# Loading the key blocks of a batch: four 32-partition transfers with a repeated source for eight of 16 partitions

## The chip, the cores and the metric

The kernel runs on one core of a Trainium2 chip. The metric is the device time of one execution in microseconds (us). The engines are TensorE (PE in the profile), VectorE (DVE), ScalarE (ACT), GpSimd (POOL) and SyncE (SP); PEld is TensorE's weight load. SP issues every transfer of this kernel, on one queue; the transfers run on 16 DMA engines. A statement of no change means within 2%.

## What is computed

Eight batches of 512 tokens with 256 features go through cross attention to 64 context tokens, and then through a mixture of eight experts. Cut to what matters:

```python
Q = (layernorm(x) @ WQ + bQ).reshape(b, 16, -1, 16)      # 16 heads of 16 features
K = (ctx @ WK + bK).reshape(b, 16, -1, 16)
V = (ctx @ WV + bV).reshape(b, 16, -1, 16)
attn = softmax(einsum('bhqd,bhkd->bhqk', Q, K) * mask) / 4
x = x + merge_heads(attn @ V) @ Wp + bp
# router: softmax over 8 experts of layernorm(x) * gamma + beta
# expert 0 has the given W1, b1, W2, b2; experts 1 to 7 share one perturbed copy
x = x + sum_e prob_e * (gelu(x @ W1_e + b1_e) @ W2_e + b2_e)
```

The experts take x as it is; only the router takes the normalised x, scaled by gamma and shifted by beta. The perturbed weights need two ranks (the largest and the smallest 5% by magnitude), which the kernel finds by a bit-by-bit search.

## The kernel before

The five engines have one hand-written program each, and semaphores join them. The main part is a loop over the eight batches (`body`, called by `pipeline`): step i finishes the attention of batch i, runs the first expert of batch i-1 beside it, does some steps of the rank search, and prepares the queries and the first three quarters of the attention scores of batch i+1. After the loop (`last_expert`) the weights are perturbed, and the second expert runs over all batches on its own.

**Where the change sits.** The scores of a batch need a block matrix of its keys, `kbd`, with 128 partitions. Its 128 rows are eight blocks of 16 rows: block 2h+n belongs to head h of a group of four. The queries were split into a high and a low part, and both parts meet the same keys; so block 2h and block 2h+1 hold the same 16 rows of `kh_scr` in HBM, at the same columns (64 to a head, for 4 groups and 2 parts of the keys: 8 runs of 64 numbers, or 256 bytes, in each row). What lies beside the blocks is zero from the start and stays so.

**SP's order.** In each step SP calls `store_queries(i+1)`, four stores of the queries to HBM (`q_scr`, L397); `load_queries(i+1)`, two loads of them in another layout (`qs`, L404), which wait until the stores have landed; and `load_context(i+1)` (L407), which loads the key blocks (`kbd`, L412), then the mask (`mk`, L416, four transfers) and the values (`vbd`, L419, two). Then come the store of the turned activations (`xt_scr`, L493) and others; the key loads of batch 0 are issued ahead of the loop. SP issues in this order, one after the other.

**Who waits for them.** `scores(b, j)` on PE (L553) waits at j = 0 for `q_in` and for `k_in`, all of a batch's key transfers. It is followed in PE's program by `router` (L637), the rest of the first expert of batch i-1 (`hidden`, `output`) and `scores(i+1, 1)` and `scores(i+1, 2)`. PE runs its instructions in order, so these stand behind the wait. `mask_scores(b, j)` on DVE (L1171) multiplies the scores with the mask and waits at j = 0 for `mask_in`; `shift` (POOL, L1062), `probs` (ACT, L866) and `turn_probs` (PE, L582) follow it. `values` (PE, L604) waits until all of a batch's scores are masked. At the switch between two rounds of the rank search DVE has a stretch of work of its own (`second_round`, L1302): between steps 2 and 3.

Of the kernel before, what the change touches and what calls it, by code (L numbers as in the profile page):

```python
# [8 lines left out]
F32 = mybir.dt.float32  # L9
# [29 lines left out]
def build_program(nc, x, ctx_in, mask, WQ, bQ, WK, bK, WV, bV, Wp, bp,  # L39
                  W1, b1, W2, b2, gamma, beta, Wr, br, out):  # L40
    B, S, D = x.shape
    CT = ctx_in.shape[1]
# [3 lines left out]
    DK = D // H  # L46
# [3 lines left out]
    HH = H // 2  # L50
# [4 lines left out]
    HG = H // 4  # L55
# [14 lines left out]
    def sb(name, shape, dt=F32):  # L70
        return ctx.enter_context(nc.sbuf_tensor(name, shape, dt))

    def sig(name, per=1):
        return Signal(ctx.enter_context(nc.semaphore(name)), per)
# [13 lines left out]
    kh_scr = nc.dram_tensor("kh_scr", [B, 4 * DK, HG, 2, CT], F32, kind="Internal").ap()  # L88
# [4 lines left out]
    def view(region, start, *shape):  # L93

        n = 1
        for d in shape:
            n *= d
        ap = region[:, start:start + n]
        if len(shape) == 1:
            return ap  # L100
        names = "abc"[:len(shape)]
        return ap.rearrange("p (" + " ".join(names) + ") -> p " + " ".join(names), **dict(zip(names[1:], shape[1:])))
# [15 lines left out]
    g = view(region_b, 2 * DC * S, 4, S)  # L118
# [68 lines left out]
    kbd = sb("kbd", [P, HG, 2, 4 * CT], F32R)  # L187
# [77 lines left out]
    keep_in = sig("keep_in", 16)  # L265
    mask_in = sig("mask_in", 16 * CC)
    v_in = sig("v_in", 32)
    k_in = sig("k_in", 16 * HH)
    q_out = sig("q_out", 2 * 16 * DC)
    q_in = sig("q_in", 2 * 16)  # L270
    ln = [dict(stats=sig(f"ln{n}_stats", NT), mean=sig(f"ln{n}_mean", NT), var=sig(f"ln{n}_var", 2),
# [50 lines left out]
    def by_query(ap, cc):  # L322

        return ap.rearrange("(r j cc) d -> cc r j d", j=NT, cc=CC)[cc]
# [24 lines left out]
    def wait(eng, signal, batch, count=None):  # L349


        value = signal.at(batch, count)
        if value > 0:
            eng.wait_ge(signal.handle, value)
# [26 lines left out]
    def _(sp):  # L381
# [25 lines left out]
        def load_context(b):  # L407
            wait(sp, s_product, b - 1)
            for h in range(4):
                for n in range(2):  # L410
                    row = (2 * h + n) * DK
                    sp.dma_start(kbd[row:row + DK, :, :, CT * h:CT * h + CT].rearrange("p g n k -> p (g n) k").bitcast(F32),  # L412
                                 kh_scr[b, DK * h:DK * h + DK].rearrange("d g n k -> d (g n) k")).then_inc(k_in.handle, 16)
            wait(sp, s_masked, b - 1)
            for cc in range(CC):
                sp.dma_start(mk[cc * R:(cc + 1) * R], by_query(mask[b], cc)).then_inc(mask_in.handle, 16)  # L416
            wait(sp, o_product, b - 1)
            for o in range(2):
                sp.dma_start(vbd[CT * o:CT * o + CT, :, DK * o:DK * o + DK],  # L419
                             v_scr[b].rearrange("t (c d) -> (t c) d", d=DK).rearrange("(g o k) d -> o k g d", k=CT, o=2)[o]).then_inc(v_in.handle, 16)  # L420
# [50 lines left out]
        sp.wait_ge(kv_out, 32)  # L471
        sp.wait_ge(eye_ready, 3)
        load_context(0)

        def put_expert(b):
# [3 lines left out]
        def body(i, rnd, first=False, last=False):  # L479
            if i + 2 < B:  # L480
                load_x(i + 2)
            load_residual(i)
            if not last:
                store_queries(i + 1)
                load_queries(i + 1)
                load_context(i + 1)
            else:

                wait(sp, o_product, i)
                sp.dma_start(wagain[:, 0].rearrange("p (c f) -> p c f", c=DC), W1.rearrange("(c p) f -> p c f", p=P)).then_inc(ld_again, 16)  # L490
                sp.dma_start(wagain[:, 1].rearrange("p (c d) -> p c d", c=FC), W2.rearrange("(c p) d -> p c d", p=P)).then_inc(ld_again, 16)
            wait(sp, x2T_ready, i)
            sp.dma_start(xt_scr[i], x2T.rearrange("p c s -> p (c s)")).then_inc(x2T_out.handle, 16)  # L493
            wait(sp, x2_ready, i)
            wait(sp, ex[0]["mixed"], i - 1)
            sp.dma_start(keep[:], x2[:]).then_inc(keep_in.handle, 16)
            if not first:
                put_expert(i - 1)
# [1062 lines left out]
```

## Time and profile before

| | |
|---|---|
| median of 3 runs | 804.89 us (800.08 to 814.68) |
| the profiled execution | 803.5 us |
| its span, first to last instruction | 801.7 us |
| granted TensorE clock, mean | 0.882 |

The span is the profiled execution without 1.8 us around it. The loop over the batches fills it from about 60 to 575 us; the second expert takes the rest. The chain of waits is followed back from the last instruction; "issue" in it is time in which an engine waited for nothing that the profile shows. A row of the timeline gives the start in us, the length in us, the engine, the line, the operation, what it writes and reads, how many instructions are merged in it, and in brackets how long the engine was idle before it and what released it.

### The profile page before, as it was taken

How to read it: one execution, taken by the hardware profiler on the slowest of the kernel's cores; microseconds unless marked ns; L12 is line 12 of the kernel's file. 1: busy time of each engine (PE TensorE's matmuls, PEld its weight loads, DVE VectorE, ACT ScalarE, POOL GpSimd, SP SyncE). 2: the span in 40 equal slices, each digit the busy share in tenths (PEclk: the TensorE clock that was granted, in tenths of full speed). 3: DMA queues.
4: the chain of work that ended last, by engine and by line, in shares of the span. 5: the costliest groups of instructions: out<-in, count | busy, mean ns of one | idle time of the engine just before them, and what ended most of it. 6: DMA issues, size and time to landing. Idle time of an engine off the chain costs nothing.

```text
span 801.7 us, 13910 instructions
## 1 busy us (share of the span) xinstructions
PE 683.7 (85%) x5442; PEld 566.5 (71%) x5442; DVE 514.0 (64%) x988; ACT 369.3 (46%) x544; POOL 228.3 (28%) x210
## 2 busy tenths in 40 slices
PE   5457777998995799898898898899987999999995
PEld 4346576886784687687687677668765888888884
DVE  5879768759669865965865874866497343343441
ACT  2214235546554554555454644545533544455442
POOL 2224034354244244334325424514280000000000
PEclk9758658989998898998797898869898999999998
DMA  9951342333153051342324206130102112222211
GB/s 279 164 134 25 54 129 54 54 102 106 19 138 105 2 111 45 107 81 75 107 38 117 80 9 147 61 124 29 68 12 80 27 53 79 80 79 79 79 32 48
DMA packets 133041, 64.40 MB, mean 80 GB/s; under 512 B 105712, under 2 KB 123120, under 8 KB 132976
## 3 DMA queue, kind: packets, MB, share of 16 engines
q1 hardware_dynamic: 132976, 63.51, 30.4%
q8 instruction: 43, 0.70, 0.4%
q14 instruction: 22, 0.18, 0.1%
HBM read 36.21 MB, written 23.09 MB: 74 GB/s over the span
## 4 chain that ended last, share of the span: by engine, by line
PE 60%; DVE 20%; issue 6%; ACT 4%; DMA 4%; SPq 3%; POOL 1%; DVEq 0%; ACTq 0%; POOLq 0%
PE ps_y L340 6%; PE ps_y L341 6%; PE ps_y L342 6%; PE ps_h L340 5%; PE ps_h L342 5%; PE ps_h L341 5%; DVE region_a L1171 3%; PE ps_t L340 3%; DVE ind L1269 3%; PE ps_m L688 3%; PE ps_t L341 3%; PE ps_t L342 3%; PE ps_t L582 3%; PE ps_t L637 2%; ACT region_a L871 2%
## 5 line engine op out<-in xcount | busy, mean ns | idle before, releaser
L1080 POOL TENSOR_TENSOR region_c_lo<-region_b,region_c_hi 128x512 fp32r<-128x512 f32 x64 | 95.7, 1504 | 117.2 <-ACT region_c_hi L910 117.2
L907 ACT ACTIVATE region_b<-ps_h,bias 128x512 f32<-128x512 f32 x92 | 63.2, 687 | 117.9 <-PE ps_h L342 116.9
L1532 DVE TENSOR_TENSOR region_c_lo<-region_b,region_c_hi 128x512 fp32r<-128x512 f32 x64 | 44.1, 692 | 107.8 <-ACT region_c_hi L910 107.8
L1269 DVE TENSOR_SCALAR ind<-key,cand 128x2048 bf16<-128x2048 uint16 x124 | 100.1, 849 | 18.2 <-PE ps_m L688 17.3
L340 PE MATMUL ps_y<-region_c_hi,w_hi 128*128 128x512 f32 x256 | 106.3, 415 | 1.9 <-POOL region_c_lo L1080 1.6
L341 PE MATMUL ps_y<-region_c_lo,w_hi 128*128 128x512 f32 x256 | 103.5, 404 | 0.0
L342 PE MATMUL ps_y<-region_c_hi,w_lo 128*128 128x512 f32 x256 | 103.0, 402 | 0.0
L1062 POOL TENSOR_TENSOR region_a<-region_a,mx 128x1024 f32<-128x1024 f32 x32 | 67.3, 2104 | 87.2 <-DVE mx L1175 87.2
L340 PE MATMUL ps_h<-x2s_hi,w_hi 128*128 128x512 f32 x184 | 81.9, 445 | 5.3 <-DVE x2s_lo L1132 4.8
L688 PEld LDWEIGHTS ps_m<-ones_bf,ind 128*128 128x128 bf16 x1984 | 56.9, 98 | 34.2 <-DVE ind L1269 24.3
L688 PE MATMUL ps_m<-ones_bf,ind 128*128 128x1 bf16 x1984 | 62.5, 164 | 20.0 <-DVE ind L1269 18.5
L342 PE MATMUL ps_h<-x2s_hi,w_lo 128*128 128x512 f32 x184 | 77.5, 421 | 0.0
L341 PE MATMUL ps_h<-x2s_lo,w_hi 128*128 128x512 f32 x184 | 77.3, 420 | 0.0
L1171 DVE TENSOR_TENSOR region_a<-ps_s,mk 128x512 f32<-128x512 f32 x64 | 40.8, 677 | 51.5 <-DMA mk<-in_mask_BxSxS_ff 35.6
L910 ACT ACTIVATE region_c_hi<-ps_h,bias 128x512 fp32r<-128x512 f32 x92 | 62.7, 681 | 0.0
L340 PEld LDWEIGHTS ps_y<-region_c_hi,w_hi 128*128 128x128 f32 x256 | 50.1, 196 | 13.9 <-POOL region_c_lo L1080 3.2
L342 PEld LDWEIGHTS ps_y<-region_c_hi,w_lo 128*128 128x128 f32 x256 | 49.6, 194 | 11.9
L341 PEld LDWEIGHTS ps_y<-region_c_lo,w_hi 128*128 128x128 f32 x256 | 50.2, 196 | 10.4
L871 ACT ACTIVATE region_a<-ps_t 128x1024 f32<-128x1024 f32 x32 | 32.8, 1024 | 41.9 <-PE ps_t L582 41.9
L566 PE MATMUL ps_s<-kbd,qs 128*128 128x256 f32 x128 | 39.3, 332 | 12.7 <-issue 9.8
L866 ACT ACTIVATE region_a<-region_a 128x1024 f32<-128x1024 f32 x32 | 33.7, 1054 | 33.2 <-POOL region_a L1062 25.2
L582 PE MATMUL ps_t<-ident,region_a 128*128 128x128 f32 x256 | 41.2, 314 | 9.1 <-ACT inv L877 4.9
(181 smaller groups left out, 1393.2 us busy)
## 6 DMA issues: line engine op xcount, KB each, us to landing
qs<-q_scr SPq DMA_DIRECT2D x16, 512.0 KB, 4.7
acc_scr<-acc SPq DMA_DIRECT2D x8, 514.0 KB, 5.1
acc<-acc_scr SPq DMA_DIRECT2D x8, 514.0 KB, 3.5
xa<-in_x SPq DMA_DIRECT2D x8, 512.0 KB, 6.0
q_scr<-qn_hi SPq DMA_DIRECT2D x16, 256.0 KB, 4.7
q_scr<-qn_lo SPq DMA_DIRECT2D x16, 256.0 KB, 5.3
x<-in_x SPq DMA_DIRECT2D x32, 128.0 KB, 4.3
xt_scr<-region_b SPq DMA_DIRECT2D x8, 512.0 KB, 2.9
```

The costliest lines, as they stand in the source:

```text
L340: eng.matmul(out_ap, a[0], b[0], start=first, stop=False)
L341: eng.matmul(out_ap, a[0], b[1], start=False, stop=False)
L342: return eng.matmul(out_ap, a[1], b[0], start=False, stop=last)
L582: mm = pe.transpose(ps_t[:, n // 4, (n % 4) * P:(n % 4 + 1) * P], pr[:, j % 2, n * P:(n + 1) * P], ident[:])
L688: mm = pe.matmul(ps_m[:, s:s + 1], ind[s % 2][:, c * P:(c + 1) * P], ones_bf[:, 0:1], start=c == 0, stop=c == WN // P - 1)
L871: act.activation(pT[:, j % 2, :], ps_t[:].rearrange("p a b -> p (a b)"), ACT.Copy).then_inc(pT_ready.handle, 1)
L907: act.activation(g[:, f % 4, :], hidden_in(e, b, f), ACT.Gelu_apprx_tanh, bias=bias[:, e, f:f + 1]).then_inc(s["gelu"].handle, 1)
L910: act.activation(gs[0][:, f % 4, :], hidden_in(e, b, f), ACT.Gelu_apprx_tanh, bias=bias[:, e, f:f + 1]).then_inc(s["g_hi"].handle, 1)
L1062: pool.tensor_tensor(m, m, mx[:, j % 2, :].unsqueeze(2).to_broadcast([P, H, CT]), ALU.subtract).then_inc(s_shifted.handle, 1)
L1080: pool.tensor_tensor(gs[1][:, f % 4, :], g[:, f % 4, :], gs[0][:, f % 4, :].bitcast(F32), ALU.subtract).then_inc(s["g_lo"].handle, 1)
L1171: dve.tensor_tensor(m[:, n * HH:(n + 1) * HH], ps_s[:, n, :].rearrange("p (h k) -> p h k", k=CT), mk[:, j, :].unsqueeze(1).to_broadcast([P ...
L1269: dve.tensor_scalar(ind[s % 2][:], key[:, key_of[rnd][s], :], cand[:, s:s + 1], None, ALU.is_le).then_inc(ind_ready.handle, 1)
```

## The change

The eight transfers of 16 partitions become four of 32. Each takes the 16 rows of one head's keys twice: the source gets a leading dimension of two with a step of zero (`unsqueeze(0).to_broadcast([2, ...])`), and the two copies go to two neighbouring blocks of 16 partitions. The same 1024 runs of 256 bytes are moved for a batch, to the same places. The semaphore `k_in` counts four transfers in place of eight. Everything else, and the order on every engine, stays as it is; SP has four instructions fewer in each `load_context`.

```diff
-    k_in = sig("k_in", 16 * HH)
+    k_in = sig("k_in", 16 * 4)
...
         def load_context(b):
             wait(sp, s_product, b - 1)
             for h in range(4):
-                for n in range(2):
-                    row = (2 * h + n) * DK
-                    sp.dma_start(kbd[row:row + DK, :, :, CT * h:CT * h + CT].rearrange("p g n k -> p (g n) k").bitcast(F32),
-                                 kh_scr[b, DK * h:DK * h + DK].rearrange("d g n k -> d (g n) k")).then_inc(k_in.handle, 16)
+                row = 2 * h * DK
+                sp.dma_start(kbd[row:row + 2 * DK, :, :, CT * h:CT * h + CT].rearrange("p g n k -> p (g n) k").bitcast(F32),
+                             kh_scr[b, DK * h:DK * h + DK].rearrange("d g n k -> d (g n) k").unsqueeze(0).to_broadcast([2, DK, 2 * HG, CT])).then_inc(k_in.handle, 16)
```

HH is 8, DK is 16, HG is 4 and CT is 64.

## Rows read from the trace of the kernel before

**Rows 1.** The page: the chain that ended last, shares of the span by engine.
```profile
PE 60%; DVE 20%; issue 6%; ACT 4%; DMA 4%; SPq 3%; POOL 1%; DVEq 0%; ACTq 0%; POOLq 0%
```

**Rows 2.** Waits of PE (57 to 575) and DVE: total us, times, longest us.
```profile
PE ps_s L604 <- DVE region_a L1171: 20.2, 7, 10.5
PE ps_s L566 <- issue: 9.8, 6, 2.1
...
DVE region_a L1171 <- DMA mk<-in_mask_BxSxS_ff: 35.6, 7, 8.0
```

**Rows 3.** Timeline of SP: start, length; the key loads of batches 0 to 7.
```profile
43.73 5.13 SPq L412 DMA_DIRECT2D kbd<-kh_scr  x8
...
93.07 4.29 SPq L397 DMA_DIRECT2D q_scr<-qn_lo  x2
...
101.41 5.64 SPq L412 DMA_DIRECT2D kbd<-kh_scr  x8
...
161.14 5.86 SPq L412 DMA_DIRECT2D kbd<-kh_scr  x8
...
226.83 5.04 SPq L412 DMA_DIRECT2D kbd<-kh_scr  x8
...
296.95 5.04 SPq L412 DMA_DIRECT2D kbd<-kh_scr  x8
...
357.90 0.87 SPq L404 DMA_DIRECT2D qs<-q_scr  x2
358.81 5.93 SPq L412 DMA_DIRECT2D kbd<-kh_scr  x8
...
424.33 5.61 SPq L412 DMA_DIRECT2D kbd<-kh_scr  x8
...
489.43 5.04 SPq L412 DMA_DIRECT2D kbd<-kh_scr  x8
```

**Rows 4.** Timeline of PE: first scores product of batches 0 to 7.
```profile
57.39 0.56 PE L566 MATMUL ps_s<-kbd,qs 128*128 128x256 f32 x1
...
108.70 0.55 PE L566 MATMUL ps_s<-kbd,qs 128*128 128x256 f32 x1 [1.44 <-DMA kbd<-kh_scr]
168.65 0.36 PE L566 MATMUL ps_s<-kbd,qs 128*128 128x256 f32 x1 [1.52 <-issue]
233.53 0.35 PE L566 MATMUL ps_s<-kbd,qs 128*128 128x256 f32 x1 [0.72 <-issue]
303.67 0.36 PE L566 MATMUL ps_s<-kbd,qs 128*128 128x256 f32 x1 [1.27 <-issue]
366.40 0.35 PE L566 MATMUL ps_s<-kbd,qs 128*128 128x256 f32 x1 [2.13 <-issue]
431.86 0.36 PE L566 MATMUL ps_s<-kbd,qs 128*128 128x256 f32 x1 [2.09 <-issue]
496.13 0.36 PE L566 MATMUL ps_s<-kbd,qs 128*128 128x256 f32 x1 [2.11 <-issue]
```

**Rows 5.** The DMA view, 360 to 364 us: busy tenths in slices of 0.1 us.
```profile
DMA  9999999999999998899999996924741100552000
```

**Rows 6.** Windows: stretch, us, busy of PE, PEld, DVE, ACT, POOL, PEclk, DMA share, GB/s.
```profile
96.00:99.00 3.00, 0.00 (x0) 0.00 (x0) 2.97 (x6) 1.24 (x2) 0.00 (x0) 0.76 0.96 147
106.00:107.00 1.00, 1.00 (x31) 0.94 (x30) 0.92 (x9) 0.54 (x1) 0.00 (x0) 0.50 0.15 33
369.00:370.00 1.00, 1.00 (x7) 1.00 (x6) 0.85 (x2) 0.00 (x0) 0.00 (x0) 0.50 0.36 39
40.50:42.50 2.00, 0.00 (x0) 0.00 (x0) 2.00 (x1) 0.00 (x0) 2.00 (x1) 0.50 0.90 192
```

**Rows 7.** Timeline: first masking of batch 3 on DVE, router on PE in steps 2 and 4.
```profile
237.50 1.29 DVE L1171 TENSOR_TENSOR region_a<-ps_s,mk 128x512 f32<-128x512 f32 x2 [3.63 <-DMA mk<-in_mask_BxSxS_ff]
...
234.56 1.84 PE L637 MATMUL ps_t<-gw,region_b 128*128 128x8 f32 x16
367.57 3.41 PE L637 MATMUL ps_t<-gw,region_b 128*128 128x8 f32 x16
```

## The prediction

> **What bounds the kernel now.** I read the chain of waits first: three fifths of the span are TensorE's work, and SP and DMA together have 7% [rows 1]. So a change to transfers matters only where PE or its suppliers wait for one. The table of waits shows such a place: PE waits in front of the first scores product (L566) seven times, and DVE waits seven times for the mask, 35.6 us in all [rows 2]. To see what ends the first of these waits I put the timelines of SP and PE beside each other. In batch 1 SP starts to issue the eight key loads at 101.41 and is done 5.64 later, at 107.05; PE starts at 108.70, 1.65 later [rows 3, 4]. In batch 5 it is 364.74 and 366.40, 1.66; over batches 1 to 7 the distance is 1.65 to 1.92. So although the profile puts six of the seven waits down to "issue", it is the landing of the last key transfer that lets PE go, in all seven batches. PE had been idle for 0.72 to 2.13 us by then, together 11.3 us [rows 4]. Measured from the start of the key issues, I for short, PE starts at I + 6.7 to 7.6 us.
>
> **What goes.** Each load_context has four issues less. Eight take 5.04 to 5.93 us, 0.63 to 0.74 each [rows 3], so about 2.5 to 3 us of SP's time go, ahead of the mask too. If nothing else changed, PE and DVE would wait less. That is the gain on offer, and it is capped by PE's 11.3 us.
>
> **What changes in the transfers.** The bytes, the 256-byte runs (one packet each) and the places are the same. What differs is the shape by which a transfer is dealt out to the 16 DMA engines. Today both sides of a key transfer begin with a count of 16 or more. The DMA view of 360 to 364 us shows, behind the query loads' full stretch, the key transfers as single short bursts that reach five tenths and more within a slice of 0.1 us [rows 5]: eight or more engines at once, so the 16 rows are spread wide. The new source begins with a count of two (step zero), the target with 32. If the shares are cut along the leading count of both sides, there are only two shares, and the same two engines get all four transfers. No row of before has a transfer with so small a leading count, so this is the unknown on which the sign hangs. I take two shares as the likelier: a split must give an engine whole steps of both sides, and a step-zero dimension of two cannot be merged with the rows behind it.
>
> Beside the rows: the Trainium skill, DMA: Bandwidth & Descriptors, section Rules for kernel authors, says that a leading zero-stride broadcast of c copies keeps a whole DMA on at most c engines. The same section advises joining small transfers into large ones, since those under 64 KB are mostly overhead, which speaks for this change (32 KB to 64 KB). By the first rule the sum is the one below, by the second that of the first rival; no run so far shows which holds here.
>
> **The price of two shares.** A batch has 1024 packets; two engines get 512 each. For the time of one packet I take a stretch in which key loads alone run: 106 to 107 us moves 33 GB/s, 129 packets of 256 bytes in the us, at a share of 0.15 of 16 engines, so 2.4 us of engine time: 18.6 ns [rows 6]. Bounds: the stores of 256-byte runs at 40.5 to 42.5 us keep the engines full at 192 GB/s, 1500 packets in 2 us, 21.3 ns of an engine's clock time each; the 128-byte stores at 96 to 99 us (147 GB/s at a share of 0.96) take 13.4 ns of engine time each. The nearest row is the first, as it is the same transfer: 512 x 18.6 ns = 9.5 us, bounds 6.9 and 10.9.
>
> **When PE can start then.** The query loads, issued just ahead, fill all engines for the first 2.3 to 2.4 us of the window at 360 us [rows 5], to about 362.3, which is I + 3.5 in batch 5. Behind them the two engines work until I + 3.5 + 9.5 = I + 13.0. From the last packet to PE's start is more than nothing and less than the 1.66 us that pass today from the end of the last issue; I take 0.7. So PE starts at I + 13.7. Against rows 3 and 4 the delays of batches 1 to 7 are 6.4, 6.2, 7.0, 7.0, 6.1, 6.2 and 7.0: 45.9 us. Batch 0 costs nothing: 43.73 + 13.7 is 57.4, when PE comes to it anyway [rows 3, 4].
>
> **What lies on the path.** PE's order puts the router, the rest of the expert and the next scores behind this wait, and DVE, POOL and ACT wait for those scores, so the shift is passed on whole, except where PE waits later for DVE and DVE was late for another reason. That is so once: of the 20.2 us for which PE waits in front of values, 10.5 are one wait [rows 2], at the switch of the search's rounds behind step 2. There DVE decides, and DVE starts on batch 3 only at 237.50, 3.97 after PE's scores begin [rows 7, 4], since it waits for the mask. The first half of the scores takes some 0.5 us, so about 3.5 of the 7.0 us are covered: minus 3.5. The mask's packets queue on the same engines behind the keys, but need only some more packets there: they land about with the scores, and I add nothing, at most 1 us a batch.
>
> **The clock.** The router took 1.84 us in step 2, after a wait of 0.72, and 3.41 in step 4, after a wait of 2.13, and the clock stood at 0.50, the lower level of 1.2 GHz, at 369 to 370 us [rows 4, 6, 7]. With waits of 8 us all steps will see the low level. Most pay it already; I add 1 us, with bounds of zero and 1.6 us for each of seven.
>
> **Sum.** 45.9 - 3.5 + 1 = 43.4 us. From the profiled execution's 803.5 us that gives 847 us; the median of the runs shown is 1.4 us higher, which I leave aside. Bounds: the packet times give 7 x (6.9 - 9.5) = -18 and 7 x (10.9 - 9.5) = +10, the landing 7 x (0 - 0.7) = -5 and 7 x (1.6 - 0.7) = +6, the clock -1 and +10; all at once is unlikely, and about 825 to 872 is the forecast's own range.
>
> **Rivals.** *All 16 engines still share a transfer* (chance 0.13). Then four issues less bring the last landing forward by 2.5 us, but PE gains no more than it idled, 11.3 us in all, so 792 at best; DVE gets the mask 2.5 us sooner too, and the queries may then land last, which I can't see in these rows. I put it at 795, within 2%. For it: the smaller issue time is certain. Against it: the leading two. It decides from the point at which a transfer uses about four engines: then the keys take I + 3.5 + 4.8 + 0.7 = I + 9, which is still late, so it needs eight or more.
> *The delay is absorbed as in batch 3* (0.08). If in every batch DVE's late mask covers 3.5 us, 7 x 3.5 of the 45.9 go: 24.5 less, 823 us. For it: DVE waits 35.6 us for the mask now. Against it: the other scores of a batch are computed behind PE's wait, and DVE needs them next.
> *SP is held by full queues* (0.05). The two stores before the query loads held SP for 4.29 us [rows 3], against 0.6 to 0.7 for an issue that goes straight through, so a long queue on two engines may hold it before the mask. If it is held to I + 13.0, the mask's four issues (2.5) and landing (1.66) end at I + 17.2: 3.5 later than PE's scores, which costs DVE up to 2 us a batch beyond the sum: 861.
>
> **Chances.** The forecast has 0.74, and the rivals 0.13, 0.08 and 0.05. A measurement of this kernel tells about 2% (16 us) from no change: slower than 821 us are the forecast and the last two rivals nearly whole, 0.85; the first rival falls within 2%, with some of the second, 0.14; faster by over 2% would need under 789, below the first rival's best: 0.01. The range 820 to 872 leaves out the first rival and some of the tails.
>
> **What would show it.** In the changed profile: SP issues four key loads in some 2.5 us or is held in them; PE's wait before L566 grows from 11.3 us to 50 or more and is put down to the key loads; in the DMA view the share sits at one or two tenths for some 9 us behind the query loads. I am wrong if the bursts still reach five tenths: then PE's wait shrinks and the time is about 795.

## The result and the profile after

| | before | changed |
|---|---|---|
| median of the runs | 802.77 us (4 runs) | 835.84 us (4 runs) |
| the profiled execution | 803.5 us | 838.5 us |
| its span | 801.7 us | 836.7 us |

The changed kernel is slower: the ratio is 1.0433, with a 95% interval from 1.0374 to 1.0492. The forecast was 847 us, in a range of 820 to 872. The medians are of all runs and the ratios of the fast runs alone, so a ratio need not be the quotient of two medians. Sign and mechanism came as forecast; three terms of the sum were off, two of them against the third.

The timelines of SP and PE of the changed kernel around batch 5 (line numbers are one lower than before, from L411 on) answer to [rows 3, 4]:

```profile
382.98 0.88 SPq L404 DMA_DIRECT2D qs<-q_scr  x2
383.89 7.11 SPq L411 DMA_DIRECT2D kbd<-kh_scr  x4
391.05 3.65 SPq L415 DMA_DIRECT2D mk<-in_mask_BxSxS_ff  x4
...
394.80 0.55 PE L565 MATMUL ps_s<-kbd,qs 128*128 128x256 f32 x1 [5.47 <-issue]
```

Four issues take 7.11 us where eight took 5.93, so SP is held in them. PE starts 10.91 us after the first of them; before, it started 7.59 after. Over batches 1 to 7 that distance is now 10.8 to 11.6, before it was 6.7 to 7.6. PE's waits show the sum (total, times, longest); they answer to [rows 2]:

```profile
PE ps_s L565 <- issue: 33.9, 6, 6.7
PE ps_s L603 <- DVE region_a L1170: 20.2, 7, 10.5
...
PE ps_s L565 <- DMA kbd<-kh_scr: 5.1, 1, 5.1
```

The seven waits in front of the first scores product are 39.0 us in place of 11.3, 27.7 more. The wait in front of values is as long as before, the one of 10.5 us included.

The windows of the changed kernel behind the query loads of batch 5 (columns as in [rows 6]) show what runs during the wait:

```profile
388.00:389.00 1.00, 1.00 (x6) 0.75 (x4) 0.48 (x2) 0.00 (x0) 0.38 (x1) 1.00 0.16 36
390.00:391.00 1.00, 0.00 (x0) 0.00 (x0) 0.00 (x0) 0.64 (x2) 0.29 (x1) 1.00 0.16 36
391.00:392.00 1.00, 0.00 (x0) 0.00 (x0) 0.00 (x0) 0.00 (x0) 0.98 (x1) 1.00 0.16 36
```

36 GB/s without a change for microseconds, at a share of 0.16, and PE at zero in the last two. The DMA view, 384 to 389 and then 389 to 394 us, 40 slices each, shows the same as a line of ones, where before there were separate bursts of five tenths [rows 5]:

```profile
DMA  8996099999999999999999996382111111111111
...
DMA  1111111111111111111111111111111111112435
```

The ones end at about 393.5, which is 9.6 us after the first key issue; the mask's bursts follow.

Of the 35 us between the two profiled executions 27.7 are these waits; the other 7.3 go with work at the lower clock. PE's busy time rose from 683.7 to 692.6 us with the same 5442 instructions. Two windows, from the first scores of batch 2 to those of batch 3 and from there to those of batch 4, show where (the last line: what follows the first scores of batch 3). First the kernel before:

```profile
168.65:233.53 64.88, 59.25 (x576) 49.62 (x577) 46.80 (x100) 34.28 (x51) 25.21 (x25) 0.89 0.32 81
233.53:303.67 70.14, 55.08 (x544) 45.25 (x545) 53.52 (x110) 33.98 (x49) 25.56 (x24) 0.90 0.30 75
...
233.53:237.53 4.00, 4.00 (x30) 3.76 (x30) 0.37 (x2) 0.00 (x0) 1.48 (x1) 1.00 0.24 44
```

and the changed kernel:

```profile
173.95:246.58 72.63, 62.25 (x576) 51.96 (x577) 46.43 (x100) 34.30 (x51) 26.01 (x24) 0.83 0.29 72
246.58:327.90 81.32, 62.16 (x544) 51.65 (x545) 52.45 (x109) 34.03 (x49) 25.37 (x24) 0.79 0.26 65
...
246.58:250.58 4.00, 4.00 (x19) 4.00 (x20) 2.57 (x4) 0.00 (x0) 0.00 (x0) 0.50 0.55 161
250.58:254.58 4.00, 4.00 (x17) 3.09 (x18) 0.10 (x2) 0.00 (x0) 3.07 (x3) 0.50 0.02 7
254.58:258.58 4.00, 4.00 (x42) 3.42 (x40) 0.26 (x2) 3.85 (x5) 1.28 (x1) 0.50 0.00 0
258.58:262.58 4.00, 4.00 (x20) 3.39 (x20) 2.30 (x9) 2.92 (x6) 0.00 (x0) 0.86 0.00 0
```

In the second stretch the same 544 matmuls take 62.16 us of PE in place of 55.08, and the stretch is 11.2 us longer, of which the longer wait at its end is 4.3. That leaves 6.9, close to the 7.1 of PE's work; the first stretch leaves 2.9 in the same way, for 3.0 of PE's work. All other stretches together leave -2.5. After the wait of 5.57 us the clock stays at the lower level (0.50) for some 13 us; after the wait of 0.72 in the kernel before it stood at 1.00.

DVE's rows behind the same scores show how the lower clock is passed on. First the kernel before, then the changed one:

```profile
240.66 0.16 DVE L1282 TENSOR_TENSOR fail<-ps_m,ranks 128x4 f32<-128x4 f32 x1 [0.48 <-PE ps_m L694]
...
250.84 1.71 DVE L1311 TENSOR_SCALAR ind<-key,prefix 128x2048 uint16<-128x2048 uint16 x2
```

```profile
247.97 1.39 DVE L1170 TENSOR_TENSOR region_a<-ps_s,mk 128x512 f32<-128x512 f32 x2 [5.89 <-DMA mk<-in_mask_BxSxS_ff]
...
255.49 0.16 DVE L1276 COPY cnt<-ps_m 128x4 f32<-128x4 f32 x1 [4.81 <-PE ps_m L687]
258.48 0.16 DVE L1281 TENSOR_TENSOR fail<-ps_m,ranks 128x4 f32<-128x4 f32 x1 [2.83 <-PE ps_m L693]
...
268.90 1.71 DVE L1310 TENSOR_SCALAR ind<-key,prefix 128x2048 uint16<-128x2048 uint16 x2
```

DVE's masking starts 1.39 us after the first scores product, where before it started 3.97 after [rows 4, 7]. But the last of the search's count products, which PE computes at the lower clock, reaches DVE 11.9 us after it in place of 7.1, and DVE's long stretch (L1311, now L1310) starts 22.3 after it in place of 17.3.

### The profile page after: what moved, and what is told of

The parts are those of the page before. It is cut to its first block, busy times and chain, and to the rows that moved or that the text cites. A ratio compares the mean times of both kernels' runs of the same rounds, so it can differ in the third digit from the quotient of the medians.

```text
span 836.7 us, 13878 instructions
## 1 busy us (share of the span) xinstructions
PE 692.6 (83%) x5442; PEld 575.9 (69%) x5442; DVE 506.4 (61%) x988; ACT 369.5 (44%) x544; POOL 229.0 (27%) x210
## 4 chain that ended last, share of the span: by engine, by line
PE 62%; DVE 19%; issue 9%; ACT 3%; DMA 3%; SPq 2%; POOL 1%; DVEq 0%; ACTq 0%; POOLq 0%
PE ps_y L340 7%; PE ps_y L341 6%; PE ps_y L342 6%; PE ps_h L340 5%; PE ps_h L342 5%; PE ps_h L341 5%; PE ps_m L687 3%; PE ps_t L636 3%; PE ps_t L340 3%; DVE region_a L1170 3%; PE ps_t L341 3%; DVE ind L1268 3%; PE ps_t L342 3%; PE ps_t L581 2%; DVE den L1178 2%
## 5 line engine op out<-in xcount | busy, mean ns | idle before, releaser
L340 PE MATMUL ps_y<-region_c_hi,w_hi 128*128 128x512 f32 x256 | 108.0, 422 | 1.7 <-POOL region_c_lo L1079 1.6
L1268 DVE TENSOR_SCALAR ind<-key,cand 128x2048 bf16<-128x2048 uint16 x124 | 96.0, 817 | 16.9 <-PE ps_m L687 15.9
L341 PE MATMUL ps_y<-region_c_lo,w_hi 128*128 128x512 f32 x256 | 105.7, 413 | 0.0
L342 PE MATMUL ps_y<-region_c_hi,w_lo 128*128 128x512 f32 x256 | 104.8, 409 | 0.0
L1170 DVE TENSOR_TENSOR region_a<-ps_s,mk 128x512 f32<-128x512 f32 x64 | 41.1, 679 | 80.3 <-DMA mk<-in_mask_BxSxS_ff 51.9
L687 PE MATMUL ps_m<-ones_bf,ind 128*128 128x1 bf16 x1984 | 62.8, 164 | 19.3 <-DVE ind L1268 17.3
L565 PE MATMUL ps_s<-kbd,qs 128*128 128x256 f32 x128 | 42.3, 351 | 39.8 <-issue 33.9
L565 PEld LDWEIGHTS ps_s<-kbd,qs 128*128 128x128 f32 x128 | 30.5, 239 | 43.4 <-issue 40.8
L341 PEld LDWEIGHTS ps_y<-region_c_lo,w_hi 128*128 128x128 f32 x256 | 51.1, 200 | 10.6
L870 ACT ACTIVATE region_a<-ps_t 128x1024 f32<-128x1024 f32 x32 | 32.8, 1024 | 39.8 <-PE ps_t L581 39.8
```

The costliest lines, as they stand in the source:

```text
L340: eng.matmul(out_ap, a[0], b[0], start=first, stop=False)
L341: eng.matmul(out_ap, a[0], b[1], start=False, stop=False)
L342: return eng.matmul(out_ap, a[1], b[0], start=False, stop=last)
L565: pe.matmul(dst, qs[:, g4, j * P:(j + 1) * P], kbd[:, g4, 0], start=True, stop=False)
L687: mm = pe.matmul(ps_m[:, s:s + 1], ind[s % 2][:, c * P:(c + 1) * P], ones_bf[:, 0:1], start=c == 0, stop=c == WN // P - 1)
L1170: dve.tensor_tensor(m[:, n * HH:(n + 1) * HH], ps_s[:, n, :].rearrange("p (h k) -> p h k", k=CT), mk[:, j, :].unsqueeze(1).to_broadcast([P ...
```

## The experiments

All times are medians, each with its ratio to the kernel before on the same chip. The intervals of the runs with four, eight and one piece and of both fillings leave out 1 but reach across 2%: their sign is clear of noise, but not that they differ by 2%.

### Is it the leading count, the repeated address, or the larger transfer?

Four kernels write the second copy of the keys to HBM once, ahead of the loop, by two transfers. LEAD is the number of pieces, with a gap of one row between them, in which the 32 source rows of a transfer lie. Number, size, target and packets of the four transfers are those of the changed kernel.

```diff
+    LR = 2 * DK // LEAD
+    kh_dup = nc.dram_tensor("kh_dup", [B, 4, LEAD, LR + (LEAD > 1), HG * 2 * CT], F32, kind="Internal").ap()
...
-                             kh_scr[b, DK * h:DK * h + DK]...unsqueeze(0).to_broadcast([2, DK, 2 * HG, CT])).then_inc(k_in.handle, 16)
+                             kh_dup[b, h, :, 0:LR].rearrange("l r (f k) -> l r f k", k=CT)).then_inc(k_in.handle, 16)
```

One piece (LEAD = 1; the rows join, and no leading count under 32 is left):

> The second copy of the keys is written to HBM once, ahead of the loop, so the four transfers keep 32 partitions, 64 KB and 256 packets each, but their source is 32 different rows in one piece and no longer begins with a count of two. Theory (a leading count of two leaves a transfer two DMA engines, and the 512 packets on each are the delay): PE starts the scores within 4.5 to 6 us of the first key issue in place of 10.9, its wait there falls from 39 us to under 10, and the time is 790 to 803 us, with up to 5 us for the copies ahead of the loop in it. Rival (fewer, larger transfers are slower as such, or hold SP): PE still starts at 9 to 11 us, 825 to 840 us.

Two pieces:

> Both copies are in HBM as in the run before, but 17 rows apart, so the source begins with a count of two again, this time without any repeated address. Theory (the count decides): as the changed kernel, PE starts 10.5 to 11.5 us after the first key issue, 830 to 843 us. Rival (reading the same HBM rows twice, or the step of zero, is what is slow): PE starts at 4.5 to 6 us, 790 to 803 us.

Four:

> The 32 source rows lie in four groups of eight with a gap between, so the source begins with a count of four. Theory: four engines get 256 packets each for a batch, 256 x 14.1 ns = 3.6 us in place of 7.2; PE starts at about 2.5 + 3.6 + 1.2 = 7.3 us after the first key issue, close to the 7.2 of the kernel before, and the time is 798 to 810 us. Rival (any gap in the source costs the same as the count of two): 10.9 us, 830 to 843 us.

Eight:

> The 32 source rows lie in eight groups of four, a leading count of eight. Theory: 128 packets on each of eight engines, 1.8 us; PE starts at 5 to 6 us after the first key issue and is then held by the query loads rather than the keys; 790 to 803 us, like the run in one piece. Rival (one piece is what matters): 830 us or more.

| leading count | time, us | ratio to before | 95% interval | PE's start after the first key issue, batch 5 | PE's waits there, batches 1 to 7 |
|---|---|---|---|---|---|
| 2, repeated (the change) | 835.84 | 1.0433 | 1.0374 to 1.0492 | 10.91 | 39.0 |
| 2, two copies | 838.88 | 1.0488 | 1.0411 to 1.0566 | 11.28 | 39.9 |
| 4, two copies | 813.49 | 1.0160 | 1.0064 to 1.0256 | 7.54 | 13.8 |
| 8, two copies | 789.77 | 0.9879 | 0.9792 to 0.9966 | 5.57 | 4.5 |
| one piece | 784.87 | 0.9733 | 0.9608 to 0.9858 | 6.23 | 3.7 |

The count decides. Without any repeated address a leading count of two is as slow as the change, and the same four transfers with their rows in one piece are faster than the kernel before. Both rivals fall. The time with four pieces lies a little above its range, the one-piece run below; the copies ahead of the loop move batch 0's keys back from 43.73 to 54.95 us in the one-piece run, where PE starts batch 0 at 59.35 in place of 57.39, so they cost it about 2 us. In the run with two pieces that price is larger: PE starts batch 0 at 64.97, 7.6 us later than before. Without them its ratio would be some 1.039, still near the change; in batches 1 to 7 PE's waits are nearly the same in both. With eight pieces PE comes to the scores of batch 5 without any wait, and its own work sets the 5.57. The rows of batch 5 with two pieces, four and eight:

```profile
388.95 7.53 SPq L415 DMA_DIRECT2D kbd<-kh_dup  x4
...
400.23 0.55 PE L579 MATMUL ps_s<-kbd,qs 128*128 128x256 f32 x1 [5.83 <-issue]
```

```profile
362.91 4.53 SPq L415 DMA_DIRECT2D kbd<-kh_dup  x4
...
370.45 0.45 PE L579 MATMUL ps_s<-kbd,qs 128*128 128x256 f32 x1 [2.10 <-issue]
```

```profile
358.13 2.89 SPq L415 DMA_DIRECT2D kbd<-kh_dup  x4
...
363.70 0.36 PE L579 MATMUL ps_s<-kbd,qs 128*128 128x256 f32 x1
```

The windows of the runs behind the query loads of batch 5 show the rates. Four pieces:

```profile
366.91:367.41 0.50, 0.50 (x4) 0.41 (x3) 0.50 (x2) 0.00 (x0) 0.49 (x1) 1.00 0.32 72
```

Eight pieces:

```profile
361.63:362.13 0.50, 0.50 (x4) 0.41 (x3) 0.46 (x6) 0.34 (x1) 0.50 (x1) 1.00 0.65 148
```

36, 72 and 148 GB/s for counts of 2, 4 and 8: the rate is proportional to the count, 18 GB/s to each share, one packet of 256 bytes in 14.2 ns. That is what one DMA engine to each step of the leading count would do; the trace doesn't name engines. The packet counts of whole executions say the same without a rate. The kernel before and the changed one:

```profile
q1 hardware_dynamic: 132976, 63.51, 30.4%
```

```profile
q1 hardware_dynamic: 132016, 63.51, 29.2%
```

The bytes are the same, and 960 packets are gone. One closing packet from each engine that takes part in a transfer would give just that: 64 transfers of 16 against 32 of two. Between the runs with one piece and with two, 132560 and 132112, the difference is 448, which is 32 times 14. What these packets are the trace doesn't say; the reading is mine.

In the one-piece run SP's four issues are through in 2.50 us, so SP is not held, and PE no longer waits for long:

```profile
350.75 0.87 SPq L408 DMA_DIRECT2D qs<-q_scr  x2
351.66 2.50 SPq L415 DMA_DIRECT2D kbd<-kh_dup  x4
...
357.89 0.36 PE L579 MATMUL ps_s<-kbd,qs 128*128 128x256 f32 x1 [0.77 <-issue]
```

This agrees with the rule cited in the prediction from the Trainium skill (DMA: Bandwidth & Descriptors, section Rules for kernel authors), with 36 GB/s for a leading count of two. The Trainium skill, on the same page in section Why a DMA increments its semaphore by 16 and not by 1, puts it more generally, as the largest number up to 16 that divides the slowest dimensions of both sides; the rates at 4 and 8 agree. The Trainium skill's advice to join small transfers (the same page, Rules for kernel authors) holds here too, once the shares are kept: one piece takes 0.9733 of the time of the eight transfers of before.

### Does the slow transfer cost anything where nobody waits for it?

The keys and the mask depend on the scores of the batch before, not on the new queries. Two kernels issue them ahead of the query stores (`load_context` then holds the keys and the mask); the value loads, now `load_values`, stay behind.

```diff
             if not last:
+                load_context(i + 1)
                 store_queries(i + 1)
                 load_queries(i + 1)
-                load_context(i + 1)
+                load_values(i + 1)
```

The changed kernel with this order:

> The changed kernel, but SP issues the next batch's key and mask loads ahead of the query stores, as soon as the scores of the batch before are computed and masked; the value loads stay behind the query loads. The four transfers still begin with a count of two and still take two engines some 7 us. Theory (the slow transfer costs time only because PE waits for it at the end of the chain of query stores and loads): the keys land some 20 us before PE needs them, PE's wait for them is gone, the queries end it, and the time is 775 to 795 us, below the kernel before. Rival (two engines kept long also slow the query stores and loads, or SP's order costs as much): 800 us or more.

The kernel before with it:

> The kernel before with the same new order on SP, eight transfers on 16 engines. Theory: as the run on the changed kernel with this order, within 1%, 775 to 795 us, since neither shape is waited for any more. Rival (the shape costs or gains in itself): the two differ by 2% or more.

They take 767.39 us (0.9602, 0.9537 to 0.9668) and 775.69 us (0.9713, 0.9649 to 0.9778). Both are under the kernel before, and the first is the fastest version here. SP's rows of the first, around batch 5 (its queries are loaded at 342.62):

```profile
312.67 6.62 SPq L411 DMA_DIRECT2D kbd<-kh_scr  x4
...
342.62 0.87 SPq L404 DMA_DIRECT2D qs<-q_scr  x2
```

SP is held by the keys for 6.62 us as in the changed kernel, but 30 us before the queries are loaded, and no wait of PE for keys or queries is left among its longest:

```profile
PE ps_s L607 <- DVE region_a L1174: 19.9, 7, 10.5
PE ps_m L691 <- DVE ind L1272: 10.7, 5, 5.7
```

So two shares for 7 us cost nothing by themselves; the loss comes from their place in the chain. The gain goes beyond the 11.3 us of PE's waits. Most of the rest goes with the clock, which falls more rarely: the profiled execution, the fastest of the four, has a mean of 0.930 for 0.882 before and 652.7 us of PE's work for 683.7, and the router takes 1.84 or 1.85 us in six of the seven steps, where before it took that in one. The mask comes early too, and DVE's 35.6 us of waits put down to it are gone; what that gives is not separated here.

Between the two shapes 1.1% is left, a little more than the 1% expected. It is under 2%, but not noise: on the same chip all four runs of the first (760.73 to 768.88) are faster than all four of the second (773.04 to 776.57). In the profiled executions 6.3 of 15.4 us lie between the first scores of batches 6 and 7, at a granted clock of 1.00 and 0.86. Why the clock differs there stays open.

### The clock behind the wait

Products by constant weights, overwritten by the scores, keep PE busy while it would wait (36 of them in the changed kernel, 12 in the kernel before):

```diff
             if j == 0:
                 wait(pe, q_in, b)
-                wait(pe, k_in, b)
                 wait(pe, x2T_ready, b - 1)
+                if b:
+                    for _ in range(36):
+                        pe.matmul(ps_s[:, 0, 0:4 * CT], wqp[0][:, 0, 0, 0:P], wqp[0][:, 0, 0, 0:4 * CT], start=True, stop=True)
+                wait(pe, k_in, b)
```

> The changed kernel with 36 products of 128 x 256 by constant weights put in front of PE's wait for the keys in batches 1 to 7; their results are overwritten by the scores. PE is busy for about 4.3 us of the 5 to 6.7 it waits. The keys land as before, at 10.9 us after their first issue. Of the profiled 35 us some 27 are PE's longer waits. Theory (the other 8 are the lower clock after the wait): the router takes 1.8 us in place of 3.4, and the time is 826 to 833 us. Rival (they are DVE's later mask and the values behind it): the time stays at 834 to 840.

> The kernel before with 12 products of 128 x 256 by constant weights in front of PE's wait for the keys in batches 1 to 7 (overwritten by the scores), about 1.4 us, so that most of its waits of 0.7 to 2.1 us are filled. The changed kernel gained some 16 us by such a filling. Theory (the clock falls after these waits already in the kernel before, in most of the batches, and the change made it fall in all): the router takes 1.8 us in all of them, and the time is 8 to 12 us under the kernel before, 786 to 795. Rival (in the kernel before the lower clock costs nothing on the path): within 3 us of it.

The filled changed kernel takes 819.53 us (1.0272, 1.0199 to 1.0344), the filled kernel before 787.94 (0.9837, 0.9756 to 0.9917). In the first the router of step 2 takes 2.06 us for 3.42 in the changed kernel:

```profile
238.30 2.06 PE L639 MATMUL ps_t<-gw,region_b 128*128 128x8 f32 x16
```

In the changed kernel it took 3.42 in all seven steps; filled, it takes 2.18 or less in six. So the clock behind this wait costs either kernel about 1.6% of the time of before, 13 us (for the kernel before, 0.8 to 2.4%). For the changed kernel that is more than the 8 us I had expected, and for the kernel before a little more than the upper end. The filling therefore doesn't show that the changed kernel pays more for the clock than the kernel before: with intervals of 0.7% on each side 6 us can't be told apart this way. That part rests on the PE busy times above alone.

### Is the late mask on the path?

In the changed kernel the mask stands behind keys for which SP is held, and DVE's waits put down to the mask grew from 35.6 to 51.9 us. One kernel issues the mask ahead of the keys:

```diff
             wait(sp, s_product, b - 1)
+            wait(sp, s_masked, b - 1)
+            for cc in range(CC):
+                sp.dma_start(mk[cc * R:(cc + 1) * R], by_query(mask[b], cc)).then_inc(mask_in.handle, 16)
             for h in range(4):
...
-            wait(sp, s_masked, b - 1)
-            for cc in range(CC):
-                sp.dma_start(mk[cc * R:(cc + 1) * R], by_query(mask[b], cc)).then_inc(mask_in.handle, 16)
```

> The changed kernel with the four mask loads issued ahead of the four key loads. Keys are issued some 2.5 us later, but their packets begin behind the query loads anyway, so PE should start the scores 0 to 1.5 us later than in the changed kernel, counted from the query loads. The mask no longer stands behind keys for which SP is held 7 us. Theory (DVE's late mask is not on the path, the scores are): 832 to 845 us. Rival (SP held by the keys, and so the late mask, costs a part of the 33 us): 815 to 828 us.

849.67 us (1.0607, 1.0540 to 1.0674): slower than the changed kernel, above the range, and far from the rival. PE's seven waits sum to 46.1 us, 7 more than in the changed kernel, and DVE now waits for the scores themselves:

```profile
PE ps_s L565 <- issue: 40.0, 6, 7.5
PE ps_s L565 <- DMA kbd<-kh_scr: 6.1, 1, 6.1
```

```profile
DVE region_a L1170 <- PE ps_s L566: 84.8, 14, 12.0
```

So the scores are on the path and the late mask gives nothing back when it comes early; issuing keys later only makes them later. The medians differ by 13.8 us, the profiled executions by 10.6: of these 7.1 are the longer waits, and PE's busy time is 3.4 longer (696.0 for 692.6) at a mean clock of 0.857 for 0.865.

## Why the prediction was right, and where its sum was off

- **What bounds the kernel.** Right: the last key transfer lets PE go. Delaying it delays the kernel (the change, two copies, mask first), advancing it speeds it up (one piece, early order).
- **Two shares.** Right, and the step that had no row now has four: counts of 2, 4, 8 and one piece, and the packet counts.
- **The price of a packet** was mis-sized: 18.6 ns, worked out from a busy share, against 14.2 ns by the rate. A share of 0.16 is 2.56 engines' time for the work of two, so the share counts more than the clock time a packet takes; packets seem to overlap on an engine. 512 packets take 7.3 us in place of 9.5. The lower bound, 13.4 ns, held it.
- **When PE can start.** Forecast at 13.7 us after the first key issue, measured 10.8 to 11.6: the keys' last packets are there at about 9.6 in place of 13.0, also because some of them move before the queries' end, and 1.3 us pass until PE starts, for which I took 0.7. So 45.9 us of delay were 27.7, PE's waits 39.0 in all where the prediction looked for 50 or more, and the ones of the DMA view last 6.0 us for its nine.
- **The 3.5 us covered in batch 3.** Right in kind, and lost again: DVE's lag behind the scores fell from 3.97 to 1.39 us, which gives 2.6. Then DVE waited for PE's count products, which ran at the lower clock, and came to its long stretch 5.0 us later, counted from the scores. PE came to its wait later by as much, so the wait of 10.5 us is as long as before. The sum let the lower clock slow PE alone, not DVE by way of PE.
- **The clock**, put at 1 us, was too small: PE's busy time grew by 8.9 us, by 7.1 behind the first scores of batch 3 alone, where the kernel before hadn't paid. The bound of 1.6 us a batch counted the router only.
- **Together**: 27.7 for 45.9, and 7.3 for the -2.5 of cover and clock, give the 35 us of the profiled executions, for 43.4 forecast. That the errors went against each other, 18.2 too much and 9.8 too little, was luck; either alone would have left the time in the range too.
- **Rivals.** All 16 engines: it didn't happen, though the one-piece run shows that this rival's gain is real, 785 us for my 795. Absorbed as in batch 3: the covering was lost again even there; besides, its 823 took batch 3's 3.5 us off twice, and 803.5 + 45.9 - 24.5 + 1 is 826. SP held: it is (7.1 us), but this is not what costs: the mask first gains nothing, and with the early order SP is held 6.62 us in the fastest version.

## What to carry to other kernels

Before transfers are joined, look at the leading count of each side: a repeat or a gap in front can leave two of 16 shares, and then fewer, larger transfers are slower. Store the repeat once, or keep the rows in one piece. Better still, issue what doesn't depend on the last step ahead of the chain that does; here that was worth more than any shape, and left about 1% between the shapes.

## What was not expected of the hardware

The same 64 KB transfers ran at 36, 72 and 148 GB/s with leading counts of 2, 4 and 8, nearly exactly in proportion. SP was held longer at its queue the smaller the count: 7.11 us for four issues with a count of two, 4.53 with four, 2.89 with eight, 2.50 in one piece. The count of packets in a whole execution fell by 960 with the bytes unchanged. Behind a wait of 5.6 us PE's clock stood at 0.50 for some 13 us of full work, and filling waits of 0.7 to 2.1 us with useless products made the kernel before 1.6% faster (0.8 to 2.4%).
